# A transformer layer on one core: where the first 128 features of half 1's attention output are projected

## The reference

```python
query, key, value = heads(...), heads(...), heads(...)      # [16, 4096, 16] each
attn = softmax(einsum('bhqd,bhkd->bhqk', query, key) / scale)
out = einsum('bhqk,bhkd->bhqd', attn, value)
out = out.transpose(0, 2, 1, 3).reshape(b, s, 256) @ Wo_w + Wo_b
x = layernorm(x + out)
x = layernorm(x + ffn(x))      # int8 weights, x rounded to int8 with one scale for the whole tensor
```

## Time and profile before

| | |
|---|---|
| median of 3 runs | 1960.79 us (1960.06 to 1961.04) |
| the profiled execution | 1961.84 us, its span in the profile 1960.0 us |
| mean granted TensorE clock | 0.982 of full speed |
| PE busy | 1864.4 us (95%) |
| ACT busy | 1801.4 us (92%) |
| DVE busy | 1574.0 us (80%) |
| POOL busy | 160.0 us (8%) |

### The profile page before, as it was taken

One profiled execution on the slowest core, in us unless ns is written; L12 is line 12 of the kernel. 1 busy time (PEld: TensorE's weight loads), 2 busy tenths in 40 slices (PEclk: granted clock), 3 DMA queues, 4 the chain that ended last, 5 costly groups with the idle time before them and its releaser, 6 DMA issues.

```text
span 1960.0 us, 31470 instructions
## 1 busy us (share of the span) xinstructions
PE 1864.4 (95%) x12996; PEld 455.1 (23%) x12996; DVE 1574.0 (80%) x1499; ACT 1801.4 (92%) x2022; POOL 160.0 (8%) x132
## 2 busy tenths in 40 slices
PE   8779999999999999999999999999999999999975
PEld 3342122122222222222222222222222122222234
DVE  4644988888888888888888888888988898888477
ACT  3239999999999999999999999999999999999955
POOL 6541800000000000000000000000000200000011
PEclk9889999999999999999999999999999999999987
DMA  5755111101111111111111111111121011111002
GB/s 166 239 178 195 25 25 25 25 20 19 21 17 25 25 25 25 25 25 26 25 28 59 17 16 26 25 25 25 25 47 25 17 18 18 24 26 25 1 24 86
DMA packets 166966, 84.15 MB, mean 43 GB/s; under 512 B 130304, under 2 KB 146944, under 8 KB 166336
## 3 DMA queue, kind: packets, MB, share of 16 engines
q1 hardware_dynamic: 162784, 75.51, 16.2%
q10 hardware_dynamic: 4032, 6.56, 1.1%
HBM read 51.48 MB, written 29.23 MB: 41 GB/s over the span
## 4 chain that ended last, share of the span: by engine, by line
ACT 61%; PE 21%; issue 10%; DVE 4%; DMA 2%; POOL 1%; SPq 0%; ACTq 0%; DVEq 0%; POOLq 0%
ACT arena L856 60%; PE PS L660 10%; PE PS L611 7%; PE PS L1141 2%; PE PS L699 1%; PE PS L1113 1%; DVE arena L916 1%; PE PS L1272 1%; DMA arena<-arena 1%; DMA arena<-xT_dram 1%; DVE bn L787 1%; DVE parts_or_sums L1528 0%; DMA k_whole<-arena 0%; POOL arena L1423 0%; POOL arena L1422 0%
## 5 line engine op out<-in xcount | busy, mean ns | idle before, releaser
L856 ACT ACTIVATE arena<-PS 128x1024 f32<-128x1024 f32 x1860 | 1708.1, 1336 | 18.5 <-PE PS L611 18.3
L660 PE MATMUL PS<-arena,Vh 128*32 128x512 f32 x8192 | 1094.6, 607 | 6.0 <-DVE arena L916 4.0
L611 PE MATMUL PS<-Qst,Kst 49*128 49x512 f16 x4096 | 727.9, 384 | 23.5 <-ACT arena L856 2.8
L916 DVE SCALAR_TENSOR_TENSOR arena<-arena 128x2048 f32<-128x2048 f32 x282 | 645.8, 2290 | 0.1
L892 DVE TENSOR_SCALAR arena<-PS 128x512 int32<-128x512 f32 x376 | 259.4, 690 | 254.4 <-PE PS L611 251.1
L611 PEld LDWEIGHTS PS<-Qst,Kst 49*128 49x128 f16 x4096 | 190.3, 93 | 1045.7 <-ACT arena L856 1018.0
L660 PEld LDWEIGHTS PS<-arena,Vh 128*32 128x32 f32 x8192 | 161.5, 108 | 314.8 <-issue 299.1
L912 DVE SCALAR_TENSOR_TENSOR arena<-arena 128x2048 f32<-128x2048 f32 x94 | 216.4, 2302 | 0.0
L900 DVE TENSOR_SCALAR arena<-arena 128x2048 int32<-128x2048 int32 x94 | 115.6, 1230 | 7.7 <-DVE arena L916 0.5
L902 DVE TENSOR_SCALAR arena<-arena 128x2048 int32<-128x2048 int32 x94 | 116.8, 1242 | 0.0
L1141 PE MATMUL PS<-arena,w 128*128 128x512 f32 x176 | 86.8, 638 | 21.9 <-DMA arena<-xT_dram 15.6
(11 more groups left out here) (118 smaller groups left out, 483.4 us busy)
## 6 DMA issues: line engine op xcount, KB each, us to landing
Kst<-k_halves SPq DMA_DIRECT2D x64, 128.0 KB
Qst<-q_halves SPq DMA_DIRECT2D x64, 128.0 KB
Vh<-head_values SPq DMA_DIRECT2D x30, 256.0 KB, 5.5
arena<-xT_dram ACTq DMA_DIRECT2D x10, 512.0 KB, 4.8
k_halves<-parts_or_sums SPq DMA_DIRECT2D x16, 256.0 KB, 2.9
k_whole<-arena SPq DMA_DIRECT2D x8, 512.0 KB, 3.8
q_halves<-parts_or_sums SPq DMA_DIRECT2D x16, 256.0 KB, 2.7
q_whole<-arena SPq DMA_DIRECT2D x8, 512.0 KB, 4.0
```

Source lines behind the costliest of these rows:

```text
L611: return nc.tensor.matmul(out, Kst[par][low:low + HK + 1, at:at + 128], Qst[par][low:low + HK + 1, j * CH:(j + 1) * CH], start=True, stop= ...
L660: last = nc.tensor.matmul(bank(value_bank(t))[32 * j:32 * j + 32, :], Vh[t % 2][:, kt, :], moving, start=kt == first, stop=kt == last_kt)
L856: nc.scalar.activation(ring(at, k), bank(g % SLOTS * SLOT, k), ACT.Exp, scale=EXP_SCALE).then_inc(a.exp, 1)
L916: last = nc.vector.scalar_tensor_tensor(out=t, in0=t, scalar=POLY[3 - j], in1=power if j == 3 else mantissa, op0=ALU.add, op1=ALU.mult)
```

## The change

The products of the first 128 features of tiles 16 to 31 are made inside the attention, one tile in each of the 16 cycles from LATE_CYCLE = 75 on (that is t = 25, kt = 31, to t = 30, kt = 31; steps 1469 to 1759). VectorE adds each to its residual tile at the end of the cycle with the same `add_first`, and the first block of the next cycle waits for that add. The schedule's steps for tiles 16 to 31 are 1469, 1488, 1507, 1528, 1546, 1564, 1585, 1604, 1622, 1643, 1662, 1681, 1702, 1720, 1738, 1759, and the next cycle's first block comes at 1471, 1489, 1508, 1529, 1547, 1567, 1588, 1606, 1624, 1645, 1663, 1682, 1703, 1721, 1741, 1762. The rows of zeros are gone. Behind the attention only the products of the other 128 features are left, each its own group, and VectorE adds them to Y as before.

```diff
+LATE_CYCLE = next(c for c in range(CYCLES) if BLOCK_STEP[QB * c + QB - 1] >= HEAD_STEP[TH + 9])
+PROJECT_IN = {(PROJECT_CYCLE + n if n < TH else LATE_CYCLE + n - TH): n for n in range(KT)}
+CYCLE_OF = {n: c for c, n in PROJECT_IN.items()}
-PROJECT_STEP = {min(BLOCK_STEP[QB * (PROJECT_CYCLE + n) + QB - 1] + 3, BLOCK_STEP[QB * (PROJECT_CYCLE + n + 1)] - 1): n for n in range(TH)}
+PROJECT_STEP = {min(BLOCK_STEP[QB * c + QB - 1] + 3, BLOCK_STEP[QB * (c + 1)] - 1): n for c, n in PROJECT_IN.items()}
...
 def project_bank(n):
-    return block_bank(QB * (PROJECT_CYCLE + n) + QB - 1)
+    return block_bank(QB * CYCLE_OF[n] + QB - 1)
...
-                if j == 0 and PROJECT_CYCLE < c <= PROJECT_CYCLE + TH:
-                    pe.wait_ge(p_added, c - PROJECT_CYCLE)
+                if j == 0 and c - 1 in PROJECT_IN:
+                    pe.wait_ge(p_added, PROJECT_IN[c - 1] + 1)
...
-                pe.wait_ge(b_bits, QB * (PROJECT_CYCLE + n + 1))
-                project_tile(n, bank(project_bank(n))[:, 0:D]).then_inc(p_proj, 1)
+                if n == TH:
+                    pe.wait_ge(a.heads[1], 16)
+                pe.wait_ge(b_bits, QB * (CYCLE_OF[n] + 1))
+                project_tile(n, bank(project_bank(n))[:, 0:D], (0, 1) if n < TH else (0,)).then_inc(p_proj, 1)
...
-        def project_tile(t, out, cs=(0, 1), starts=True, stops=True):
+        def project_tile(t, out, cs=(0, 1)):
             for c in cs:
                 last = nc.tensor.matmul(out, heads_out(t // TH, c, t % TH * 128, 128),
-                                        w[:, W_O + c * D:W_O + (c + 1) * D], start=c == 0 and starts, stop=c == 1 and stops)
+                                        w[:, W_O + c * D:W_O + (c + 1) * D], start=c == cs[0], stop=c == cs[-1])
...
-                if 0 <= c - PROJECT_CYCLE < TH:
-                    add_first(dve, c - PROJECT_CYCLE)
+                if c in PROJECT_IN:
+                    add_first(dve, PROJECT_IN[c])
                 split_bits(dve, c)
...
             pe.wait_ge(fast.exp, STEPS_ALL)
-            pe.wait_ge(fast.heads[1], 16)
             pe.wait_ge(b_bits, QB * CYCLES)
-            late = TH + 2 * value_bank(NT - 1)
-            for t in [t for t in range(TH, KT) if t not in (late, late + 1)] + [late, late + 1]:
-                if t == late:
-                    pe.wait_ge(fast.norm, NORM0 + NSTEP * (NT - 1) + 1)
-                if t % 2 == 0:
-                    nc.tensor.matmul(bank(t % TH // 2), identb[0:1, :], zero_row[:, :], start=True, stop=False)
-                project_tile(t, PS[:, t % TH * D:(t % TH + 1) * D], (0,), starts=False)
+            pe.wait_ge(fast.norm, NORM0 + NSTEP * (NT - 1) + 1)
             pe.wait_ge(fast.heads[1], 16 * 2)
             pe.wait_ge(fast.last, 16 * 2 * QB)
             for t in range(TH, KT):
-                last = project_tile(t, PS[:, t % TH * D:(t % TH + 1) * D], (1,), stops=t % 2 == 1)
+                last = project_tile(t, PS[:, t % TH * D:(t % TH + 1) * D], (1,))
```

More of the change, by code:

```diff
@@ L217 @@
 STEP = {p: n + 1 for n, p in enumerate(make_vector_steps())}
-assert len(PROJECT_STEP) == TH and NORM_BLOCK + TH + 8 < QB * CYCLES
+assert len(PROJECT_STEP) == KT and NORM_BLOCK + TH + 8 < QB * CYCLES
 KR = 6 * HD
```

## The result

The changed kernel is slower by a little: 1964.7 us median of 20 runs (1960.64 to 1966.95) against 1960.35 us of the kernel before (20 runs, 1956.73 to 1962.91), a ratio of 1.0023 with a 95% interval of 1.0016 to 1.0030, or +4.35 us. The forecast was 1962.1 us and "no change"; the measured time lies in the range, on the slow side. The ratio stands just past the 0.2% that was taken as no change, with an interval that reaches to both sides of it, and +4.35 us is over three times the +1.3 of the forecast. So the interest lies in the terms: the sum was 2.9 us lost inside the attention and 1.6 us gained behind it.

A forecast was written before the change was run, and what follows sets the result against it. ScalarE was taken as the bound inside the attention, with little TensorE time to spare. Losses of 1.6 + 0.8 + 0.5 = 2.9 us inside, less 1.6 gained behind, gave +1.3: median 1962.1 us, range 1958.3 to 1966.0.

The forecast's parts named there:

- Behind the attention: Behind the attention: the pass starts 3.4 us sooner, the low clock takes 1.8 us of it, 1.6 us gained.
- C: Behind the attention: the low clock holds for the whole pass, 0.5 us lost, not 1.6 gained; 1964.2 us, chance 0.13.
- D: Behind the attention: the pass starts no sooner, the landing being its limit already; 2.9 us lost, 1963.7 us, chance 0.02.
- The products inside: Inside the attention: 16 tiles take 8.5 us of TensorE, slack takes up 6.9, 1.6 us lost.
- 2 or 3 exponentials fewer in 300 us: Inside the attention, sign of being right: ScalarE does that many fewer exponentials in the cycles with the moved products.
- Adds and the block's wait: Inside the attention: the next cycle's first score block waits until VectorE has added the tile; 0.5 us lost.
- Rival B: Inside the attention: the block waiting for the add holds TensorE's queue, then ScalarE; 8.2 us lost, 1967.4 us, chance 0.12.
- The stall: Inside the attention, 1550 to 1600 us: VectorE lacks idle time, its delay adds to TensorE's existing wait; 0.8 us lost.
- Rival A: Inside the attention: the smaller tiles fit whole into TensorE's slack, and the clock costs little; 1958.3 us, chance 0.15.

The follow-up runs named there:

- e2: The changed kernel with 13 products of no use put into TensorE's gap behind the attention; 1961.72 us, ratio 1.0007 to the kernel before.
- e12: e6 with the product of each tile 16 to 31 made in two pieces of 128 columns, one step apart; 1967.98 us, executed once.
- e10: e6 without VectorE's adds of tiles 16 to 31 and the block's wait for them, products only; 1959.06 us, executed once.
- e13: The kernel before without the 8 rows of zeros behind the attention, and nothing else; 1956.7 us, ratio 0.9980.
- e11: e6 without the products of tiles 16 to 31 inside the attention, adds and wait only; 1958.26 us, executed once.
- e6: The changed kernel with the two maxima of half 0 moved behind the last projection; 1960.61 us, ratio 1.0001 to the kernel before.
- e7: The kernel before with the two maxima of half 0 moved to the same later blocks, 364 and 368; 1958.57 us, ratio 0.9990.

## Why the prediction was right or wrong, point by point

**Behind the attention: right.** That the last heads' landing is the next limit (7.4 us of idle expected, 7.27 measured), that the gap lowers the clock, that two pairs then run at half rate and VectorE hides the rest (the first add 1.95 us behind the first matmul expected, 2.09 measured; the second 1.70 later, expected 1.77; the last add 1.6 us sooner expected, 1.7 measured). What e2 undid is what was charged for the clock, 1.8 us. That it was just two pairs is in part luck: with the same gap, the last add of e12 comes 0.3 us sooner and that of e10 0.5 us later than the changed kernel's. And the one case that the forecast leant on, the 2.00 us stall of the earlier trace rows, is no rule: e13 has the same stall and keeps its clock (below). The rule of the Trainium skill's page "TensorE: Matmul & The Clock Gate", section on HAM oscillation, held here: the granted clock was 0.53 and 0.62 behind the gap, and 1.00 with the gap filled. Rivals C and D are out: the clock rose during the pass, and the pass did start sooner. What the forecast had not in view is the other way to the same gain, e13: the first products fit into the wait for the last heads once the zero rows are gone.

**The products inside: the step that failed.** The prediction says "0.53 us of TensorE each, 8.5 in all", and leaves 1.6 us. Measured: 0.63 us each, 10.1 in all, and 3.7 us lost (e10). The half of a 1.06 us group is not the time of one of its two members, as the first one carries 0.20 us of its own. The second half of the step, slack (spare time of TensorE) that takes up 6.9 of 17.0 us, came from counting 11 exponentials; by the starts of the records heads 17 to 22 took 330.1 us against six times 53.17, so 11.1 us were lost and 5.9 taken up, 0.37 us a tile. With these two numbers the same reasoning gives 10.1 - 5.9 = 4.2 us, near the 3.7. The sign "2 or 3 exponentials fewer in 300 us" failed with it: it was six in 320. The mechanism, a slack and the rest lost, was right; the size was off by a factor of over two, inside the bounds given (none to 5.0).

**Adds and the block's wait: right in kind, small in size.** 0.5 us was taken, e11 shows 1.2, and the profile 1.3 us in three waits of L614 for L952. Rival B (8.2 us inside) is out: 5.4 were lost, and TensorE waited for an add at three more places, not at eight; e11 shows the cost at heads 25 and 26.

**The stall: too much.** 0.8 us was taken. TensorE's wait did grow by 0.65 us, as foreseen, but with the maxima away the difference of the two kernels fell only from 5.44 to 5.22 us, less than the clock's chance at head 26. Perhaps TensorE and ScalarE were themselves later by then, so that VectorE's delay was only in part a new one; no run separates that. The prediction also had the tiles off by one: it puts tile 18's add just before the stretch from 1550 to 1600, and it came in it, at 1552.98.

**The sum.** 1.6 + 0.8 + 0.5 = 2.9 us was forecast inside and 5.4 measured, 1.6 gained and 1.7 measured: +3.7 us by the traces, +4.35 by the times (3.1 to 5.9 by the interval), +1.3 forecast. Rival A is out: the smaller tiles didn't fit into the slack whole. The chance of 0.84 on "within 0.2%" leant mostly on the term of the products, which was too small. The time stayed in the range because the range reached past rival C into B, not because its centre was near.

What stays open: why TensorE's stream needs the extra 0.20 us when it goes over from value products or scores to the fp32 product. The weight load in front of it is the suspect, and nothing here separated it. Nor did I try fewer tiles inside (only those whose block follows later); by e6 and e7 each tile costs some 0.3 us inside and saves 0.43 behind only while the landing isn't the limit, which after e13 it is.

## What to carry to other kernels

Before moving work from the end into the steady part, see what the end waits for next: here 11 us of work could give back 3.6, and nearly as much of it was overhead (the zero rows, and the breaks that they made between the products) that could be dropped where it stood. Work that filled a wait for a transfer was free here, and in e2 it even paid, as it kept TensorE's clock up. Where two engines are within 2% of each other, the spare time is small and doesn't grow with what is moved: here it was some 6 us over 16 cycles, with 0.63 as with 1.06 us a tile. Take it off once and charge the rest nearly in full. And take the time of moved work in the place where it will stand, alone, not as a share of a longer group.

## What the runs showed of the hardware that I had not expected

- A product of fp32, 128 by 128 by 256, put singly between other matmuls, takes 0.63 us of TensorE, two in a row 1.06, half the columns 0.42, and 16 in a row 7.17 (0.45 each).
- The clock need not fall behind a stall of 2 us: with the same attention code and the same stall the kernel before shows 3.4 us of low clock at head 26 and e13 none, and head 26 is then 56.35 and 55.72 us. In e13:

```profile
1562.84 1.07 PE L660 MATMUL PS<-arena,Vh 128*32 128x512 f32 x8 [2.00 <-issue]
...
1560.00:1564.00 4.00, 1.87 (x14) 0.40 (x14) 4.00 (x3) 3.14 (x4) 4.00 (x6) 1.00 0.13 52
1564.00:1568.00 4.00, 4.00 (x35) 0.79 (x33) 3.79 (x6) 3.44 (x4) 4.00 (x4) 1.00 0.11 44
```

- The last stretch, from the first transposes to the end, takes 41.6 or up to 43.1 us for the same code, as the granted clock is back at 1.00 between 3.2 and 6.3 us behind its start; these 1.5 us are a quarter of the spread of the 20 runs of the kernel before.
